# The last 21 tiles of a wavelet block: one butterfly stays in PSUM, GpSimd adds the whole of x, cells get two buffers, and the ring for output and x gets four

## The reference

```
ll, lh, hl, hh = haar_dwt(x)                         # four 80x80 bands
fused = relu(bn(conv1x1(concat(ll, lh, hl, hh))))    # 1024 -> 256 channels
sp = sigmoid(conv7x7(mean and max of fused over channels))
gated = sp * fused
ch = sigmoid(mlp(mean over pixels) + mlp(max over pixels))
proj = relu(bn(conv1x1(ch * gated)))                 # 256 -> 1024 channels
out = haar_idwt(proj in four bands) + x
```

## Time and profile before

| | |
|---|---|
| median of 3 runs | 2567.86 us (2566.55 to 2569.47) |
| the profiled execution's own time | 2566.07 us |
| its span | 2564.3 us |
| PE busy | 2429.5 us, 95% |
| DVE busy | 2066.0 us, 81% |
| POOL busy | 388.1 us, 15% |
| tail, from DVE's first cells of tile 91 to the end | 2256.9 to 2564.3 us |

### The profile page before, as it was taken

The page is one execution under the profiler, slowest core; times in us unless marked ns, Lnnn a source line. Parts: engine busy times, 40 slices in busy tenths (PEclk is TensorE's granted clock), DMA queues, the critical chain, the costliest instruction groups (busy, mean ns, idle before and its releaser), DMA issues. The chain is left out here.

```text
span 2564.3 us, 32151 instructions
## 1 busy us (share of the span) xinstructions
PE 2429.5 (95%) x12373; PEld 2121.6 (83%) x12373; DVE 2066.0 (81%) x2611; ACT 1072.1 (42%) x1421; POOL 388.1 (15%) x347
## 2 busy tenths in 40 slices
PE   5999999999999999999999999999999999986886
PEld 4888889898898978888898888989888888975765
DVE  4756778797778887788787987788877888779898
ACT  3444534354344533455334543445434453324222
POOL 0010111111111111111111111111111111122233
PEclk9999999999999999999999999999999999988999
DMA  4445699999999999999999999999999999886687
GB/s 142 159 159 178 183 279 273 269 294 262 253 276 272 294 254 258 281 273 285 261 265 271 287 271 271 270 274 292 256 260 268 281 291 258 232 286 243 247 289 281
DMA packets 110301, 660.26 MB, mean 257 GB/s; under 512 B 15362, under 2 KB 16452, under 8 KB 109892
## 3 DMA queue, kind: packets, MB, share of 16 engines
q1 hardware_dynamic: 83940, 487.80, 50.1%
q0 software_dynamic: 26208, 170.41, 36.5%
HBM read 448.04 MB, written 210.12 MB: 257 GB/s over the span
## 5 line engine op out<-in xcount | busy, mean ns | idle before, releaser
L483 PE MATMUL pp<-y_hi,wp_hi 128*128 128x480 f32 (+1 forms) x1792 | 677.4, 378 | 75.5 <-DVE y_lo L824 45.2
L746 DVE TENSOR_TENSOR x_lo<-xin,x_hi 128x1920 fp32r<-128x1920 f32 (+1 forms) x224 | 461.9, 2063 | 318.9 <-ACT x_hi L576 318.8
L576 ACT ACTIVATE x_hi<-xin 128x1920 fp32r<-128x1920 f32 (+1 forms) x224 | 418.1, 1867 | 671.1 <-PE pf L497 671.1
L497 PE MATMUL pf<-x_hi,wf_hi 128*128 128x480 f32 (+1 forms) x1792 | 677.7, 378 | 11.3 <-DVE wp_lo L741 6.2
L483 PE MATMUL pp<-y_lo,wp_hi 128*128 128x480 f32 (+1 forms) x1792 | 671.0, 374 | 0.0
L483 PE MATMUL pp<-y_hi,wp_lo 128*128 128x480 f32 (+1 forms) x1792 | 668.6, 373 | 0.0
L497 PE MATMUL pf<-x_hi,wf_lo 128*128 128x480 f32 (+1 forms) x1792 | 665.3, 371 | 0.0
L497 PE MATMUL pf<-x_lo,wf_hi 128*128 128x480 f32 (+1 forms) x1792 | 664.7, 371 | 0.0
L483 PEld LDWEIGHTS pp<-y_hi,wp_hi 128*128 128x128 f32 x1792 | 341.6, 191 | 133.9 <-DVE y_lo L824 61.1
L606 ACT ACTIVATE relu<-pp,t 128x480 f32<-128x480 f32 (+1 forms) x448 | 285.1, 640 | 397.3 <-PE pp L483 357.2
L801 DVE SCALAR_TENSOR_TENSOR xre<-sd,both 128x960 f32<-128x960 f32 (+1 forms) x364 | 410.3, 1169 | 6.5
(11 more groups left out here) (89 smaller groups left out, 1180.7 us busy)
## 6 DMA issues: line engine op xcount, KB each, us to landing
xin<-in_x_dram SPq DMA_DIRECT2D x160, 960.0 KB, 6.7
out_dram<-xre SPq DMA_DIRECT2D x160, 960.0 KB, 5.2
xre<-in_x_dram POOLq DMA_DIRECT2D x130, 960.0 KB, 9.3
xin<-in_x_dram SPq DMA_DIRECT2D x64, 800.0 KB, 6.5
out_dram<-xre SPq DMA_DIRECT2D x64, 800.0 KB, 4.5
xre<-in_x_dram POOLq DMA_DIRECT2D x52, 800.0 KB, 8.9
xre<-in_x_dram SPq DMA_DIRECT2D x30, 960.0 KB, 6.6
sigb<-sig_scratch SPq DMA_DIRECT2D x56, 400.0 KB, 7.9
```

What stands on the lines that cost most here:

```text
L483: mm = pe.matmul(pp[j][:, 0:n_px], w[:, kt, cols], y[:, s.pc, kt, 0:n_px], start=(kt == 0 and m == 0), stop=(kt == CT - 1 and m == 2))
L497: mm = pe.matmul(pf[o][:, 0:n_px].rearrange("p (y w) -> p y w", w=W2), w[:, i, q, o * P:(o + 1) * P], v[:, q % 2, :, q // 2, :], start=(i ...
L576: nc.scalar.activation(halves(x_hi, i, k), pairs(i, k), ACT.Copy).then_inc(xhi_ready[i], 1)
L746: nc.vector.tensor_tensor(halves(x_lo, i, k), pairs(i, k), halves(x_hi, i, k).bitcast(F32), ALU.subtract).then_inc(xlo_ready[i], 1)
```

## The change

For the tail alone: (1) the second butterfly (n = 1) is written to PSUM, into `pfs`, the two banks that the fusion used (`pf`), so that `cells` reads one operand from SBUF and one from PSUM; (2) DVE adds no x any more, and GpSimd adds all 1920 elements of a half (`sum_x`), without the waits for `lo_ready` and `mult_done`; (3) `cell` gets two buffers, which lie where `xin` was, and cells wait for the sum before last instead of the last; `last_gate` moves from `xin` to `x_lo`; (4) the ring `xre` has four slices instead of three, for all tiles. SBUF use stays the same.

```diff
+    RING = 4
-        xre = sb("xre", [P, 3, XPM])
+        xre = sb("xre", [P, RING, XPM])
-        cell = sb("cell", [P, XPM])
+        cell = xin
+        last_gate = [v[:, :, :].rearrange("p a b -> p (a b)").bitcast(F32)[:, 0:NPX // 2] for v in (x_lo, x_hi)]
+        pfs = ctx.enter_context(nc.psum_tensor("pfs", [P, 1024], F32))
+        pf = [pfs[:, j * 512:(j + 1) * 512] for j in range(2)]
...
-        def residual(eng, ops, kc, i, hand, added):
-            g = 2 * kc + i
-            n = 2 * px_of(kc)
-            part_of = slice(hand * n, (hand + 1) * n)
-            eng.wait_ge(xre_landed[g % 3], 16 * uses(g, False))
-            eng.wait_ge(cell_ready, 2 * (g + 1))
-            x_part = xre[:, g % 3, part_of]
-            ops.tensor_tensor(x_part, x_part, cell[:, part_of], ALU.add).then_inc(added, 1)
...
@@ store
-                    sp.wait_ge(added_v, plain_upto(g))
-                    sp.wait_ge(added_p, plain_upto(g))
+                    sp.wait_ge(x_summed, plain_upto(g))
...
@@ gpsimd
+            def sum_x(kc, i):
+                g = 2 * kc + i
+                x = xre[:, g % RING, 0:4 * px_of(kc)]
+                gp.wait_ge(xre_landed[g % RING], 16 * uses(g, False))
+                gp.wait_ge(cell_ready, 2 * (g + 1))
+                nc.gpsimd.tensor_tensor(x, x, cell[:, g % 2, 0:4 * px_of(kc)], ALU.add).then_inc(x_summed, 1)
...
-                        if not s.load_next and s.phase and s.phase - 1 in GATED:
-                            gp.wait_ge(mult_done, CT * (NCH * s.nb + GATED[s.phase - 1][1] + 1))
-                        residual(gp, nc.gpsimd, s.kc - 1, 1, 1, added_p)
+                        sum_x(s.kc - 1, 1)
...
-                    elif s.c_next and not s.next_is_first:
-                        gp.wait_ge(lo_ready, CT * (s.kn + 1))
-                    if not s.load_next and s.phase in GATED:
-                        gp.wait_ge(mult_done, CT * (NCH * s.nb + GATED[s.phase][0] + 1))
-                    residual(gp, nc.gpsimd, s.kc, 0, 1, added_p)
+                    sum_x(s.kc, 0)
...
@@ vector
+            def butterfly(s, i, n):
+                both_rows = slice(0, 2 * px_of(s.kc))
+                return pfs[:, both_rows] if n == 1 and not adding(s.kc, i) else sd[:, n, both_rows]
...
-                    need(dve, added_v, plain_upto(g - 1))
-                    need(dve, added_p, plain_upto(g - 1))
-                    to = cell[:, 0:4 * n_px]
+                    dve.wait_ge(xlo_ready[CT - 1], NT)
+                    need(dve, x_summed, plain_upto(g - 2))
+                    to = cell[:, g % 2, 0:4 * n_px]
...
-                    if not s.c_is_first and not adding(s.kc - 1, 1):
-                        residual(dve, nc.vector, s.kc - 1, 1, 0, added_v)
...
-                    if not adding(s.kc, 0):
-                        residual(dve, nc.vector, s.kc, 0, 0, added_v)
```

More of the change, by code:

```diff
@@ L235, in haar_block @@
         cell_ready = sem("cell_ready")
[L236 to L240, removed]
+        x_summed = sem("x_summed")
+        xre_landed = [sem(f"xre_landed{p}") for p in range(RING)]
+        x_added = [sem(f"x_added{p}") for p in range(RING)]
+        stored = [sem(f"stored{p}") for p in range(RING)]
         LL, LH, HL, HH = range(4)
@@ L269, in uses @@
         def uses(g, by_dma):
-            return sum(adding(*divmod(n, 2)) == by_dma for n in range(g % 3, g + 1, 3))
-        def residual(eng, ops, kc, i, hand, added):
-            g = 2 * kc + i
-            n = 2 * px_of(kc)
-            part_of = slice(hand * n, (hand + 1) * n)
-            eng.wait_ge(xre_landed[g % 3], 16 * uses(g, False))
-            eng.wait_ge(cell_ready, 2 * (g + 1))
-            x_part = xre[:, g % 3, part_of]
-            ops.tensor_tensor(x_part, x_part, cell[:, part_of], ALU.add).then_inc(added, 1)
+            return sum(adding(*divmod(n, 2)) == by_dma for n in range(g % RING, g + 1, RING))
         block = ctx.enter_context(nc.Block())
@@ L311, in load_residual @@
                     sp.wait_ge(wf_psum, 4)
[L312 to L313 removed]
+                need(sp, stored[g % RING], 16 * (g // RING))
+                sp.dma_start(xre[:, g % RING, 0:4 * px_of(kc)], dram(x_v, kc, i)).then_inc(xre_landed[g % RING], 16)
             def store(kc, i):
@@ L378, in _ @@
             store(NT - 1, 1)
-            for p in range(3):
-                sp.wait_ge(stored[p], 16 * len(range(p, 2 * NT, 3)))
+            for p in range(RING):
+                sp.wait_ge(stored[p], 16 * len(range(p, 2 * NT, RING)))
         @block.gpsimd
@@ L426, in body @@
                 elif s.c:
[L427 to L433 removed]
+                    sum_x(s.kc, 0)
             for s in slots:
                 body(s)
[L437 removed]
+            sum_x(NT - 1, 1)
         @block.tensor
@@ L772, in butterflies @@
                     dve.wait_ge(blockmax_ready, s.k + 1)
+                if not adding(s.kc, i):
+                    dve.wait_ge(f_ready, CT * NT)
                 for n, j in enumerate((LL, HL)):
@@ L775, in butterflies @@
                     dve.wait_ge(r_ready, 2 * g + 1 + n)
-                    rows = sd[:, n, 0:2 * n_px].rearrange("p (y e w) -> p y e w", e=2, w=W2)
+                    rows = butterfly(s, i, n).rearrange("p (y e w) -> p y e w", e=2, w=W2)
                     p = pp[j][:, 0:n_px].rearrange("p (y w) -> p y w", w=W2)
@@ L866, in body @@
                 if ahead:
-                    if s.c and not s.c_is_first and not adding(s.kc - 1, 1):
-                        residual(dve, nc.vector, s.kc - 1, 1, 0, added_v)
                     dve.wait_ge(logit_psum, s.nb + 1)
@@ L918, in _ @@
                 body(s)
-            residual(dve, nc.vector, NT - 1, 1, 0, added_v)
 _INS = ["x"] + ["L0_conv_" + n for n in (
```

21 lines of the change are left out of this document (8 added, 13 removed).

## The result

The changed kernel takes 2626.57 us (median of 4 runs, 2625.0 to 2627.54), the kernel before 2568.66 us beside it (4 runs, 2566.55 to 2572.24). The ratio is 1.0224, 95% interval [1.0209, 1.0240]: slower. The forecast was 2619 us, the range 2594 to 2640. The profiled execution took 2627.54 us and its span is 2625.7, so that 61.4 us more span are to be found. That is 3.5 us more than the 57.9 between the medians, since the profiled execution of the kernel before (2566.07 us) was faster than all its timed runs, and that of the changed kernel is the slowest of its four.

The account below looks back on a forecast made before the run. PE bounds the kernel before the tail, DVE's chain the tail. Terms -1 + 18 + 3 + 23.5 + 9 - 1 = 51.5 us on 2566.1 give 2617.6, with 1.8 for the median 2619; range 2594 to 2640.

Parts of the forecast that it names:

- DVE's chain: Tail slots: 13.49 us falls by 2.24 to 11.25; 26 us gained over 11.5 slots if nothing else moved.
- GpSimd gets in between the two `lower` instructions: Slots 120 to 131: DVE's pair takes 5.7 us instead of 1.34, price 4.3 a slot; net +23.5 us.
- A gate is blocked too: Slots 115 to 117: the second gate step, behind half 1's cells, costs another 4.3 us; +18 in all.
- PE's lowered clock: Slots 120 to 131: PE idles 5 us, then runs at 1.2 GHz; 0.8 us a slot (bounds 0 and 1.2), +9.
- Slot 114: Its second gate step finds x late and passes unblocked; slots 112 to 114 together -1, or +4 if blocked.
- PSUM operands cost nothing: Tail: DVE's 84 PSUM writes and 84 reads add nothing; upper bound 18 us.
- The ring of four: Main part: DVE's cells never had to wait for a slice, so four slices change nothing.
- SP's queue covered: Tail: sum, store, load and landing take 11.9 us a slot, under 15.5, so they add nothing.
- rival A: Tail: DVE keeps the port, no blocks; slots 11.25 or 11.9 us, -30 in all, 2538 us; chance 0.07.
- Slots 118 and 119: Terms of -1 for 118, and +1 and +3.2 for 119; together +3 us.
- B: Tail: GpSimd gets in at `lower` but not at a gate, and the clock holds; +30, 2598 us; chance 0.10.
- C: Dearer tail: full clock +5, slot 114 blocked +4, PSUM writes +9, 2637 us; 2651 if cells contend; chance 0.10.

Follow-up runs that it names:

- e9_load_first: e1 with SP issuing each load of x ahead of the store before it, in slots 120 to 132 and once in slot 111; 2528.63 us.
- e1: The changed kernel with GpSimd's waits for lo_ready and mult_done put back in front of the sum; 2544.63 us.
- e3: The changed kernel, no waits, with GpSimd's sum as two instructions of 960 elements instead of one of 1920; 2577.46 us.
- e8: The kernel before, with GpSimd's waits for lower and gate taken out and nothing else changed; 2606.54 us.
- e4: The changed kernel with 14 matmuls that nobody reads, issued past slot 120 while PE waits for y_lo; 2610.68 us.
- e7: e1 with a ring of three slices instead of four; 2545.02 us.
- e10: e9_load_first with a ring of three slices instead of four; 2599.56 us.
- e11: The changed kernel, without GpSimd's waits, with SP's order of loads and stores from e9_load_first; 2630.19 us.
- e2: The changed kernel with only GpSimd's wait for lo_ready put back; 2567.57 us.

## Why the prediction was right, and where its sizes were off

- **DVE's chain is the bound, and becomes 11.25 us: right.** e9_load_first shows it to the hundredth, and its slots 120 to 131 gain 25.9 us, the 26 that the prediction gave "if nothing else moved".
- **GpSimd gets in between the two `lower` instructions: right**, in every slot of the tail past 120, by e1 (2544.63 without the blocks), e3 and e8. The price was taken as 4.3 and is 4.0 (5.34 - 1.34): 1920 elements are 4.34 us, not 4.5, and GpSimd has the port 0.48 us after the pair's start (0.23 + 0.25), not 0.71.
- **A gate is blocked too: right** (5.08 us). Slots 115 to 117 cost 16.2 us, forecast 18; with blocks of 4.03 the same sum gives (2 x 4.03 - 2.24) x 2.83 = 16.5.
- **PE's lowered clock: right in kind, the largest miss in size.** I took 0.8 us a slot, bound 1.2. It is 17.1 / 11.5 = 1.5, and e4 gives 16.5 / 11.5 = 1.4. Two steps failed. The discount from 1.2 to 0.8, for slots in which the clock would not fall in full, was read off the gate slots of before; here it falls in all twelve. And the 3.9 us at 1.2 GHz, read from one place of before, are 4.8 on average here (5.0 to 5.8 in eight slots, 3.4 in four). One us at that level costs PE 1 - 0.22/0.40 = 0.45 us, so 0.9 us more are 0.4 on the bound: 1.6 a slot, near what was measured. The trace of before had longer stretches than 3.9, the eighth column again the granted clock:

```profile
2331.48:2338.31 6.83, 6.29 (x19) 5.70 (x19) 6.74 (x11) 0.78 (x2) 2.23 (x1) 0.50 0.51 207
```

  The term gives 17 and not 9; the shorter block takes 3 back, and slots 120 to 131 come out 4.7 above the forecast. PE's idle time before `project` is 3.8 us and not the 5 forecast, since PE ends its last half 7.8 us into the slot (2439.02) and not at 5.4.
- **Slot 114: wrong side taken.** I let its second gate step pass unblocked, with 4 us more if not. x landed as that step began: 2.7 instead of -1.
- **PSUM operands cost nothing: right.** Cells take 2.34 us a pair with `pfs` and 2.35 with both in SBUF. The Trainium skill, VectorE: DVE Perf Modes, section The TRN2 errata, has a higher fixed cost for a PSUM source; no row here shows it.
- **The ring of four: nothing, right** for the change's order of SP's queue (e7), and only for it (e10).
- **SP's queue covered: right** (e11). Without the blocks it is not: rival A's 11.9 a slot by sum, store and load compares with a mean of 12.1 in e1_waits_back (139.50 / 11.5), made of slots at DVE's 11.25 and of longer ones, up to 13.94, and its 2538 with 2544.63.
- **Slots 118 and 119** cost 4.0 instead of 3, slot 132 nothing instead of -1, and the first tail slot began 1.3 us later; between the kernels run here that start differs by up to 8 us (2256.87 in before, 2265.03 in e10_load_first_ring3), so I give it no cause.
- **One reading was off:** rows 4 show the cells 0.03 us behind the butterfly's end stamp, not 0.1. By that GpSimd would come 0.11 us after `lower` has started; the forecast's 0.2 is near the measured 0.23 by luck.
- **How much of the nearness is luck.** The sum was 51.5 us and the profiles have 61.4. Above the forecast are the clock (8), slot 114 (3.7), the start of the tail (1.3), slots 118 and 119 (1) and slot 132 (1); below it is the shorter block (3.4 past slot 120, 1.8 in the gate phases). Without this last, which has nothing to do with the others, the forecast would have been 15 us off in these spans and not 10.

Rival A, that DVE keeps the port, and B, that a gate is spared, are refuted. C was half true: its clock and its slot 114 (+9) came, its PSUM cost and contending cells did not, and 2619 + 9 = 2628 is near the 2626.57, in part because what its clock is too low by and what its blocks are too dear by cancel. Why the lower clock comes at once and lasts 5 us or more in eight slots, and comes later and lasts 3.4 us in four, stays open, and so does what lets a waiting GpSimd in between two vector instructions that lie back to back.

## What to carry to other kernels

A semaphore wait that seems to delay an idle engine may be what keeps its instruction from landing between two instructions of the critical one: before taking it out, find what it starts beside, and price a collision at the whole other instruction, plus what the stall does to the engine behind (here 4.0 us of block and 1.4 us of clock a slot). Work moved to GpSimd paid, 24 and then 40 us, once each sum started behind the instructions with two SBUF operands, once those that it does meet had one operand in PSUM, and once it had a second buffer. A deeper ring is worth something only if the queue issues loads ahead of the stores that they used to follow; look at the order and the depth together.

## What the runs showed of the hardware that was not expected

- The instruction that reads the accumulator (0.08 us) between two gate instructions is no shield: the second is stamped as started at once and takes 5.04 to 5.10 us instead of 0.98 (after, e2, e11; 800 pixels beside a sum of 1920 elements).
- Splitting one GpSimd sum of 4.34 us into two of 2.27 halves the block (3.31 us for the pair instead of 5.34), since DVE gets its turn between the two.
- 14 matmuls of no use made the kernel 15.9 us faster, by a clock of 0.96 instead of 0.82.
- A store was done only 8.2 us after its issue, as seen by a queue that stands for it (e10_load_first_ring3), where stores of this size in e9_load_first have a median of 4.7.
